# Head-masked key blocks of an attention layer, made by ScalarE straight from PSUM instead of by GpSimd for each pair

## The reference, cut to what matters

```python
q = split_heads(layernorm(x) @ Wq.T + bq)
k = split_heads(ctx @ Wk.T + bk)
v = split_heads(ctx @ Wv.T + bv)
scores = where(mask == 0, -1e9, einsum('bhqd,bhkd->bhqk', q, k) / sqrt(8))
x = x + (softmax(scores) @ v, heads joined) @ Wo.T + bo
# router: logits = x @ Wr + br; expert = argmax; gate = its probability
# y = gate * (relu(layernorm(x) @ W1[expert] + b1) @ W2[expert] + b2)
out = x + y
```

## Time and profile before

| | |
|---|---|
| runs | 316.54 us median (315.61, 316.54, 317.49) |
| profiled execution | 319.22 us, span 317.5 us, mean granted TensorE clock 0.915 |
| TensorE matmul busy | 249.2 us (79%) |
| VectorE busy | 220.6 us (70%) |
| ScalarE busy | 177.3 us (56%) |
| GpSimd busy | 141.2 us (44%), 33.2 us of it L365 (32 times, mean 1042 ns) |
| L423 | 8 times, mean 675 ns |

### The profile page before, as it was taken

The page is one execution under the profiler, slowest core; times in us unless marked ns, Lnnn a source line. Parts: engine busy times, 40 slices in busy tenths (PEclk is TensorE's granted clock), DMA queues, the critical chain, the costliest instruction groups (busy, mean ns, idle before and its releaser), DMA issues.

```text
span 317.5 us, 8922 instructions
## 1 busy us (share of the span) xinstructions
PE 249.2 (79%) x3112; PEld 200.7 (63%) x3112; DVE 220.6 (70%) x674; ACT 177.3 (56%) x342; POOL 141.2 (44%) x158
## 2 busy tenths in 40 slices
PE   1488988998979989789898665008899999899880
PEld 0336665765857767658576664007788888788870
DVE  6517864785886979958798735814877877877870
ACT  1527784777584767576655310007667667667640
POOL 3812250541456476464672617720444434444441
PEclk9999997997997999999999955556999999999996
DMA  7999999999999940000000101111122121121110
GB/s 228 298 245 223 273 232 238 253 265 261 263 294 267 255 109 22 10 23 15 11 28 2 37 0 37 43 40 39 43 49 59 54 68 42 51 67 53 48 29 0
DMA packets 49611, 36.31 MB, mean 114 GB/s; under 512 B 3087, under 2 KB 45460, under 8 KB 49568
## 3 DMA queue, kind: packets, MB, share of 16 engines
q1 hardware_dynamic: 46864, 31.11, 43.3%
q0 software_dynamic: 2272, 4.27, 4.2%
q10 hardware_dynamic: 432, 0.38, 0.5%
HBM read 14.11 MB, written 22.09 MB: 114 GB/s over the span
## 4 chain that ended last, share of the span: by engine, by line
PE 38%; DVE 31%; issue 14%; ACT 5%; DVEq 3%; DMA 3%; POOL 2%; POOLq 1%; SPq 1%; ACTq 0%
PE ps L742 8%; PE ps L753 7%; DVE Pr L569 5%; PE ps L729 4%; DVE mx L549 4%; DVE xh L685 4%; DVE hT L697 4%; PE ps L803 3%; DVE ot L706 3%; PE ps L760 2%; PE ps L766 2%; PE ps L725 2%; PE ps L780 2%; DVE yb L704 2%; DVEq L674 2%
## 5 line engine op out<-in xcount | busy, mean ns | idle before, releaser
L388 POOL DMA_INDIRECT out<-ot,G x39 | 39.8, 1021 | 62.6 <-DVE ot L706 61.6
L415 ACT ACTIVATE PT<-ps 128x512 f32<-128x512 f32 x64 | 35.2, 595 | 49.7 <-PE ps L753 49.6
L549 DVE TENSOR_REDUCE mx<-ps 128x16 f32<-128x1024 f32 x32 | 39.2, 1224 | 28.6 <-PE ps L729 28.1
L742 PEld LDWEIGHTS ps<-VB,PT 128*64 128x64 f32 x1024 | 34.1, 140 | 27.1 <-issue 27.1
L742 PE MATMUL ps<-VB,PT 128*64 128x18 f32 x1024 | 36.9, 214 | 14.7 <-ACT OT L408 7.3
L834 PE MATMUL ps<-xg,WR 128*128 128x128 f32 x312 | 45.1, 289 | 0.0
L845 PE MATMUL ps<-WR,hT 128*128 128x128 f32 x312 | 41.0, 275 | 0.0
L365 POOL TENSOR_TENSOR Kb<-KT,hmask 128x512 f32<-128x512 f32 x32 | 33.2, 1042 | 17.0 <-PE ps L729 16.7
L419 ACT ACTIVATE Pr<-Pr,rowany 128x1024 f32<-128x1024 f32 x32 | 36.7, 1148 | 7.1 <-DVE Pr L569 6.0
L834 PEld LDWEIGHTS ps<-xg,WR 128*128 128x128 f32 x312 | 39.2, 197 | 1.4
L341 POOL DMA_INDIRECT rows_dram<-row,posi x32 | 32.5, 1016 | 14.3 <-DVE row L582 6.5
(11 more groups left out here) (121 smaller groups left out, 379.7 us busy)
## 6 DMA issues: line engine op xcount, KB each, us to landing
rows_dram<-empty SPq DMA_DIRECT2D x32, 528.0 KB, 10.5
WA<-in_wpk SPq DMA_DIRECT2D x8, 578.0 KB
G<-rows_dram SPq DMA_DIRECT2D x39, 66.0 KB, 1.9
X<-in_x SPq DMA_DIRECT2D x8, 256.0 KB, 7.2
C<-in_ctxT SPq DMA_DIRECT2D x8, 256.0 KB, 6.6
XT<-in_xT SPq DMA_DIRECT2D x8, 256.0 KB, 6.5
out<-ot,G POOLq DMA_INDIRECT x39, 2.3
rows_dram<-row,posi POOLq DMA_INDIRECT x32
```

What stands on the lines that cost most here:

```text
L388: g.indirect_dma_start(out=out, out_offset=bass.IndirectOffsetOnAxis(ap=G[:, q, D + 1:D + 2].bitcast(I32), axis=0), in_=ot[:, q, :], in_of ...
L415: a.activation(PT[:, p % 2, 512 * m:512 * m + 512], ps[:, 4 + m, :], ACT.Copy).then_inc(freed[4 + m], 1)
L549: v.tensor_reduce(out=mx[:, i % 2, :], in_=psS.rearrange("p g (i k) -> p g i k", k=S), axis=AX.X, op=ALU.max).then_inc(s_mx, 1)
L742: last = mm(psPV[64 * b:64 * b + 64, 18 * j:18 * j + 18], PT[:, p % 2, 128 * j + 64 * b:128 * j + 64 * b + 64], VB[:, p // GP % 3, 2 * (p ...
```

## The change

`KT` and the GpSimd product go. ScalarE reads the K product out of PSUM four times, each time with a per-partition scale `hmask[:, n]` and a per-partition bias `bkm[:, n]` = `bk * hmask[:, n]`, and writes the four masked blocks of the whole group, in two buffers by group. `bkm` is one small operation on VectorE, once. The scores product of a pair reads its columns from the group's buffer and waits for the evacuation, not for GpSimd; the evacuation waits for the scores of the last pair of the group before the previous one, and once for `bkm`. The next fill of bank 7 waits for the fourth evacuation.

```diff
-        KT = sb("KT", [P, 2, GP * P])
-        Kb = sb("Kb", [P, 3, 4, P])
+        Kb = sb("Kb", [P, 2, 4, GP * P])
+        bkm = sb("bkm", [P, 4])
...
-                if 0 <= i + 2 < NP:
-                    p = i + 2
-                    pool.wait_ge(freed[7], nth("k", p // GP))
-                    wait(pool, s_cdve, 3 if p == 0 else 0)
-                    wait(pool, s_s, p - 2)
-                    c = P * (p % GP)
-                    g.tensor_tensor(out=Kb[:, p % 3, :, :],
-                                    in0=KT[:, p // GP % 2, c:c + P][:, None, :].to_broadcast([P, 4, P]),
-                                    in1=hmask[:, :, None].to_broadcast([P, 4, P]), op=ALU.mult).then_inc(s_kb, 1)
...
                 if (gr := group_at(i, 5)) is not None:
                     act.wait_ge(filled[7], nth("k", gr))
-                    wait(act, s_kb, GP * (gr - 1))
-                    a.activation(KT[:, gr % 2, :], ps[:, 7, :], ACT.Identity, bias=bk).then_inc(freed[7], 1)
+                    wait(act, s_s, GP * (gr - 1))
+                    wait(act, s_cdve, 4 if gr == 0 else 0)
+                    for n in range(4):
+                        last = a.activation(Kb[:, gr % 2, n, :], ps[:, 7, :], ACT.Identity, bias=bkm[:, n:n + 1],
+                                            scale=hmask[:, n:n + 1])
+                    last.then_inc(freed[7], 1)
...
                                 op=ALU.max).then_inc(s_cdve, 1)
+                dve.wait_ge(s_wa, 16)
+                dve.wait_ge(s_cdve, 3)
+                v.tensor_scalar(bkm[:], hmask[:], bk, None, ALU.mult).then_inc(s_cdve, 1)
...
                     pe.wait_ge(freed[7], nth("q", i // GP))
-                    pe.wait_ge(s_kb, i + 1)
+                    pe.wait_ge(freed[7], nth("k", i // GP))
...
-                                      Kb[32 * j:32 * j + 32, i % 3, :, 64 * b:64 * b + 64],
+                                      Kb[32 * j:32 * j + 32, q, :, c + 64 * b:c + 64 * b + 64],
```

More of the change, by code:

```diff
@@ L194, in build @@
             "ln1_stats", "ln1_moments", "ln1_var_eps", "ln1_rstd", "ln1_shift", "xn"))
-        s_kb, s_xb, s_s, s_mx, s_sub, s_p = (sem(n) for n in (
-            "k_blocks", "x_plus_bo", "scores", "row_max", "softmax_shift", "probs"))
+        s_xb, s_s, s_mx, s_sub, s_p = (sem(n) for n in (
+            "x_plus_bo", "scores", "row_max", "softmax_shift", "probs"))
         s_rc, s_st2, s_ag2, s_ve2, s_rs2, s_nm2 = (sem(n) for n in (
```

## The result

| | before | after |
|---|---|---|
| median of 4 runs | 316.85 us (315.61 to 317.49) | 324.36 us (322.15 to 324.78) |
| profiled execution | 319.22 us, span 317.5 | 324.78 us, span 323.0 |
| mean granted clock | 0.915 | 0.922 |

The ratio is 1.0228 [1.0171, 1.0285]: slower, by 7.2 us, where +2.7 was forecast and the range ended at 321.7. The mean of the four is 1.016, about +5 us. So the direction was right, the size was too low, and the first measurement is the highest of four. Executions more than some 1.5% above the fastest of their kernel don't count in any ratio of this document, while a profile can be of such a one.

What follows compares the result with a forecast made beforehand. The bound was taken as a per-step cycle of TensorE scores and VectorE maximum and subtraction, stretched by group work. 2.14 + 0.9 + 1.16 - 1.5 = +2.7 us on the 316.54 median gave 319.2 us, range 316.2 to 321.7.

Steps and rivals of the forecast that it cites:

- Term 1: At the start, group 0's four K evacuations delay every piece behind them: +2.14 us, bounds +1.74 and +2.41.
- the shift under 1.5 that would have made it wrong: Sign of error: the first row maximum, forecast to move from 22.34 to near 24.5, moving by under 1.5 us.
- Term 2: Group 1's K evacuations hold up its V product: 0 or 1.8 us by TensorE's clock, taken as +0.9.
- Term 3: Groups 2 to 7: V waits for late K evacuations, 0.89 us in group 2, 0.11 in 6, 0.16 in 7: +1.16.
- Term 4: Attention part: without GpSimd's product, a 2.36 us VectorE instruction no longer collides with it and `xb`: -1.5 us, bounds 0 and -2.2.
- No engine on the chain waits for them in the attention part: GpSimd's `xb` and scatters, no longer gated by scores, come up to a step earlier; claimed to hold up no chain engine.
- the new `bkm` on VectorE I cost at nothing: At the start, one more small VectorE operation, covered by a wait for GpSimd: no cost, 0.2 us if the cover failed.
- the expert part as long as before: Sign expected in the changed profile: the expert part, behind the attention part, keeps its length.
- Hidden after all: Rival: better overlap, clock up in time, collision gain full 2.2 us: +0.0 to +1.5, 316.6 to 318.1 us; chance 0.22.
- Fewer falls of the clock: Rival: shifted group phases remove two or three of the attention part's three clock falls: 315.8 or 314.1 us; chance 0.15.
- ScalarE becomes the bound: Rival: evacuations of one bank don't overlap and the collision gains nothing: 322 to 323 us; chance 0.11.

Runs made afterwards that it cites:

- hyb_from3: ScalarE's four evacuations only in groups 3 to 7, GpSimd's product kept in groups 0 to 2, against the kernel before: 1.0114 [1.0047, 1.0181].
- after_fourth: The changed kernel unaltered, measured again beside the kernel before on the same chip: 1.0113 [1.0039, 1.0187].
- after_bkm_act: The changed kernel with `bkm` made on ScalarE instead of VectorE, against the kernel before: 1.0108 [1.0045, 1.0172].
- after_pool2: The changed kernel with GpSimd's product put back into a tile nobody reads, against the kernel before: 1.0155 [1.0074, 1.0236].
- dve_stream: The kernel before with one small VectorE operation added, with its two waits, into a tile nobody reads: one execution, 321.08 us.
- act_stream: The kernel before with three single-column ScalarE instructions added per group, into a tile nobody reads: one execution, 330.04 us.
- the two halves measured singly: The change in groups 0 and 1 alone, 1.0111, and in groups 2 to 7 alone, 0.9992, each against the kernel before.
- unbound: The changed kernel, but K evacuated once and ScalarE writing the four masked blocks from SBUF, against the kernel before: 1.0436 [1.0354, 1.0518].
- the one-line reorder: The kernel before with GpSimd's `xb` addition one step earlier, nothing else, against the kernel before: 0.9911 [0.9861, 0.9961].
- after_third: The changed kernel unaltered, measured a third time beside the kernel before on one chip: 1.0174 [1.0124, 1.0225].
- after_again2: The changed kernel unaltered, measured a second time against the kernel before: 1.0138 [1.0076, 1.0199].

## Why the prediction was right in sign and low in size

**Term 1, +2.14: right.** The first maximum is at 24.3 to 24.5 in every profile with four evacuations at the start and at 22.15 to 22.34 in all but one without (22.95 in `hyb_from3`): +2.0 to +2.3. The price (0.77), the overlap and the 2.81 held; the shift under 1.5 that would have made it wrong was far off.

**Term 2, +0.9 as the middle of 0 and 1.8: right as a term with two ends.** Eight profiles have the four evacuations in group 1 and nothing in the gap. V ran slow in five (second maximum 5.2 to 5.4 us behind the first) and fast in three (3.75 to 3.83), so it costs 1.6 or 0 at that point. Over the first four pairs it is 1.5 to 2.3 in the five and 0 to 0.4 in the three, 1.2 in the mean. The middle was a mean, not a value that a run takes. The Trainium skill (TensorE: Matmul & The Clock Gate, What's actually happening) has the gate run free of the kernel; the changed kernel, slow in two of its profiles and fast in two, agrees. The prediction's reading of it, 1.8 each time, doesn't hold.

**Term 3, +1.16: right for group 2, wrong in the late groups.** Group 2 cost 0.73 (19.42 against 18.69 where neither has a fall) for the 0.89 forecast. Groups 3 to 5 cost nothing beyond what the clock does. For the 0.11 and 0.16 of groups 6 and 7 no wait is in after; on the three chips named above V of group 7 waits 0.68 us, and pairs 24 to 28 take 2.1 us longer without GpSimd's product. In after pairs 12 to 20 took 20.5 us for each four in place of 19.8 with no fall of the clock; single long steps of that kind are in `after_fourth` and `after_bkm_act` too, and stay open.

**Term 4, -1.5: right.** The pairs from 20 to 24 went from 21.50 to 19.81, -1.7, with L594 at 0.36 at most. Added up over L583, L594 and L620, VectorE loses 2.7 us above the usual length in after, where it lost 4.4 in before. `after_pool2` shows the cause. But new collisions were left out of the sum. "No engine on the chain waits for them in the attention part", said of `xb` and the scatters that come earlier, was wrong: in after `xb` holds up L583, and pairs 24 to 31 took 0.5 us longer or more in every changed kernel without the product.

**The step that failed: "the new `bkm` on VectorE I cost at nothing", and with it "the expert part as long as before".** I asked only what hides the operation's own 0.2 us, and was right there: ScalarE starts at 9.19 in place of 9.13. I didn't ask what one more instruction does to the engine's stream behind it. With it slot 13 is 0.5 us longer, and slots 34 and 37 wait for `out` stores: +0.4 to +1.1 us in three profiles of the changed kernel, +4.0 in the first, 2.8 of them in the slots behind the store of 4.42 us. That slots 13, 34 and 37 come from this operation is shown in the traces (`dve_stream` has them, `act_stream` and `after_bkm_act` don't). That the late store does, and that the operation explains the whole excess over 2.7, isn't; in time it couldn't be told apart (1.0108 without it, 1.0113 with it).

**The sizes put together.** 2.1 + 1.2 + 0.7 + 0.5 (pairs 24 to 31) - 1.7 = +2.8 for the attention part, and the slots make it +3.2 to +3.9; the two halves measured singly, 1.0111 x 0.9992, give +3.3, with the weakness of the second. The four measurements of the whole have a mean of +5. Between 1 and 2 us isn't settled; the spread of the four (1.0113 to 1.0228), the differences between chips, the late `out` stores and `hyb_from3` say how much chance one comparison holds.

**The rivals.** "Hidden after all" fell with the first maximum. "Fewer falls of the clock" came true in the profile, one in the attention part where there were three, and still the time was longer; over all executions the low time is no shorter for before. "ScalarE becomes the bound" gives the time closest to the first measurement but by the wrong route: neighbours overlap as assumed (2.78 for four), and groups 3 to 6 show no wait in after. `unbound` comes nearest to it.

## What to carry to other kernels

Work taken from an engine that nobody waits for buys only its collisions; find these first (one instruction far above its group's mean, with both its inputs in SBUF), and add them up over all instructions afterwards, for both the change and the one-line reorder moved some of them elsewhere. An evacuation that gates a product at the start or behind an idle gap costs its full length, so three more ahead of it are three more on the path, and where they stand in the queue can matter more than what each takes. Where a change is worth 1%, measure it several times, on more than one chip, and in separately run halves, and compare stages far from the edit too: one instruction more on an engine can move pauses 230 us later.

## What the runs showed of the hardware that was not expected

- An ACTIVATE of 128x512 from PSUM with scale and bias both per partition takes 772 ns, four in a row 2.77 to 2.78 us; three further tiny ones in each group cost nothing in the slots.
- The same 32 products of V take 1.98 or 1.15 us at the same place of the same kernel, behind the same 1.25 us of idle time.
- TensorE can stay at its lower level for most of 14 us with 12.4 us of it busy (`after_third`), and as long in `after_again2` and `act_stream`; most other falls before 160 us last under 4 us. These four pairs took 8.7 us more than in `after_fourth`.
- The indirect store of `out`, for which a later gather waits, was seen on the chain with 2.85, 3.13, 3.78, 4.04 and 4.42 us from issue to landing.
- GpSimd's `xb`, freed of the product ahead of it, doubled a VectorE instruction with two SBUF inputs at 161 us (0.42 to 0.91 us); the product put back restored it.
- One added VectorE instruction at the start, with its waits, lengthens an "issue" wait of the same engine in slot 13 from 0.48 to 0.83 us and takes that of slot 33 away; neither 6160 bytes more in SBUF nor 24 more ScalarE instructions do.
